# Two attention layers: all jobs in new orders, with row-major score jobs of different 32-row groups side by side

## The reference

```
# layer 0, per batch: channels on 128 rows, 256 positions, 16 heads of width 8
q = layer_norm(x + pos) @ Wq;  k, v = layer_norm(ctx + pos) @ Wk, Wv
probs = softmax(q k^T / sqrt(8));  x += (probs v) @ Wo;  then layer norm and a gelu feed-forward
# layer 1, per batch: 128 queries, 256 keys (context, then the tokens themselves), 16 heads of width 16
scores = q k^T * scale + mask;  x = rmsnorm(x + softmax(scores) v @ out_w);  then a gelu feed-forward
```

## Time and profile before

| what | value |
| --- | --- |
| median of 3 runs | 2342.38 us (2339.53 to 2348.45) |
| the profiled execution's own time | 2341.19 us |
| its span in the trace | 2339.3 us |
| PE busy | 2192.3 us, 94% of the span |
| DVE, ACT, POOL busy | 1476.0, 1316.3, 684.5 us |
| first layer's attention, PE at work | 13.3 to 335.4 us |
| second layer's attention, PE at work | 368.4 to about 645.2 us |

### The profile page before, as it was taken

One profiled execution on the slowest core, in us unless ns is written; L12 is line 12 of the kernel. 1 busy time (PEld: TensorE's weight loads), 2 busy tenths in 40 slices (PEclk: granted clock), 3 DMA queues, 4 the chain that ended last, 5 costly groups with the idle time before them and its releaser, 6 DMA issues. The chain is left out here.

```text
span 2339.3 us, 48273 instructions
## 1 busy us (share of the span) xinstructions
PE 2192.3 (94%) x18208; PEld 1805.4 (77%) x18208; DVE 1476.0 (63%) x2833; ACT 1316.3 (56%) x3812; POOL 684.5 (29%) x652
## 2 busy tenths in 40 slices
PE   6999978999888999999999999999999899999989
PEld 4666646777677888888888888888887786776778
DVE  5778743444463666566666766666666538999963
ACT  4777753454443544444445444444444549999953
POOL 4443312111170423030211503030101506677740
PEclk9999998999989999999999999999999899999999
DMA  4000002000011101010100001010000201000000
GB/s 131 16 15 11 2 1 55 2 2 2 2 37 46 39 25 37 1 46 1 30 17 10 30 17 37 1 37 1 1 1 1 109 21 37 2 2 2 2 10 28
DMA packets 33666, 50.62 MB, mean 22 GB/s; under 512 B 2592, under 2 KB 22048, under 8 KB 32416
## 3 DMA queue, kind: packets, MB, share of 16 engines
q1 hardware_dynamic: 33440, 47.53, 6.5%
HBM read 45.43 MB, written 2.10 MB: 20 GB/s over the span
## 5 line engine op out<-in xcount | busy, mean ns | idle before, releaser
L633 ACT ACTIVATE l_probs<-l_s_psum,l_neg_max 128x129 f32<-128x129 f32 x512 | 181.4, 367 | 266.3 <-DVE l_neg_max L696 266.3
L720 DVE TENSOR_TENSOR x<-x,l_o_psum 128x512 f32<-128x512 f32 x256 | 176.1, 688 | 189.1 <-PE l_o_psum L587 187.4
L2524 ACT ACTIVATE l_probs<-l_probs,l_neg_max 128x128 f32<-128x128 f32 x512 | 210.9, 534 | 0.0
L618 ACT ACTIVATE l_KT<-l_k_psum,cols 128x512 f32<-128x512 f32 x128 | 88.2, 689 | 196.9 <-PE l_k_psum L114 196.9
L465 POOL TENSOR_TENSOR l_head_w_high<-l_head_raw,one 128x768 fp32r<-128x768 f32 x30 | 44.5, 1482 | 516.2 <-PE l_o_psum L587 516.2
L1232 DVE TENSOR_REDUCE l_neg_max<-l_psum 128x2 f32<-128x512 f32 x256 | 164.5, 683 | 48.5 <-PE l_psum L1024 48.4
L2354 POOL TENSOR_TENSOR l_probs<-l_probs,l_mask_add 128x512 f32<-128x512 f32 x128 | 162.0, 1286 | 78.6 <-DVE l_probs L2582 78.6
L1163 ACT ACTIVATE l_PT<-l_psum 128x512 f32<-128x512 f32 x256 | 132.1, 603 | 56.5 <-PE l_psum L1052 53.8
L587 PE MATMUL l_o_psum<-l_head_w_high,l_context_low 128*128 128x256 f32 x512 | 155.8, 304 | 8.5 <-DVE l_context_low L701 8.5
L701 DVE SCALAR_TENSOR_TENSOR l_context_low<-l_c_psum,cols,l_context_high 128x512 fp32r<-128x512 f32 x128 | 95.8, 749 | 105.3 <-ACT l_context_high L625 104.5
L2524 ACT ACTIVATION_READ_ACCUMULATOR l_probs<-l_probs,l_neg_max 128x1 f32 x512 | 155.2, 334 | 0.0
(11 more groups left out here) (303 smaller groups left out, 6600.2 us busy)
## 6 DMA issues: line engine op xcount, KB each, us to landing
l_head_raw<-in_l_heads SPq DMA_DIRECT2D x32, 384.0 KB, 2.9
l_w<-in_l_w SPq DMA_DIRECT2D x4, 1024.0 KB, 9.8
l_ctx_in<-in_ctx_T SPq DMA_DIRECT2D x16, 256.0 KB, 5.5
l_value_raw<-in_l_values SPq DMA_DIRECT2D x8, 512.0 KB, 3.5
l_value_rows<-in_l_rows SPq DMA_DIRECT2D x8, 512.0 KB, 5.0
l_x_in<-in_x_T SPq DMA_DIRECT2D x16, 128.0 KB, 2.1
l_x_in<-in_ctx_T SPq DMA_DIRECT2D x16, 128.0 KB, 2.5
values<-in_l_w SPq DMA_DIRECT2D x2, 1024.0 KB, 5.9
```

The source lines that it names most:

```text
L633: last = act.activation(probs[:, i, :], scores[:, i // 2, i % 2, :], ACT.Exp, bias=neg_max[:, i:i + 1], scale=1.0, accum_out=den[:, i:i + 1])
L720: dve.tensor_tensor(out=x, in0=x, in1=o_bank[:, :], op=ALU.add).then_inc(o_free, 1)
L2524: last = act.activation(p, p, ACT.Exp, bias=neg_max[:, s % SCORES3, m:m + 1], scale=1.0, accum_out=den[:, u % 2, 4 * r + m:4 * r + m + 1])
```

## The change

Both tables get new numbers; no job is added, removed or altered. The core of the diff:

```diff
 AT0 = {
-    "rows": (0.62, 0.63, 0.68, 0.74, 0.77, 0.8, 0.84, 0.84,
-             0.86, 0.89, 1.02, 1.08, 1.17, 1.27, 1.3, 1.32),
+    "rows": (-0.69, -0.6899, -0.57, -0.5699, -0.48, -0.4799, -0.32, -0.3199,
+             -0.29, -0.2899, -0.27, -0.2699, -0.09, -0.0899, 0.09, 0.0901),
...
 AT1 = {
-    "rows": (-3.3, -2.91, -2.87, -2.6, -2.47, -2.4, -2.33, -2.33),
+    "rows": (-4.97, -4.95, -4.34, -4.25, -4, -4, -4, -4),
...
-    "neg_T_a": (-2.51,),
+    "neg_T_a": (-4.18,),
...
-    "exponents": (-2.48, -2.36, -2.35, -2.27, -2.03, -1.51, -1.51, -1.51),
+    "exponents": (-4.15, -4.11, -3.97, -3.97, -3.18, -3.18, -3.18, -3.18),
```

More of the change, by code:

```diff
@@ L762 @@
 AT0 = {
[L763 to L774, removed]
-    "rows": (0.62, 0.63, 0.68, 0.74, 0.77, 0.8, 0.84, 0.84,
-             0.86, 0.89, 1.02, 1.08, 1.17, 1.27, 1.3, 1.32),
[L777 to L799, removed]
+    "place": (-4.97,),
+    "stats": (-3.77,),
+    "root": (-3.79,),
+    "scaled": (-1.91,),
+    "normed": (-1.6,),
+    "normed_a": (-1.23,),
+    "project": (-0.98,),
+    "project_a": (-0.54,),
+    "round": (-1.43,),
+    "blocks": (-0.94,),
+    "value": (-0.72,),
+    "values": (-0.55,),
+    "rows": (-0.69, -0.6899, -0.57, -0.5699, -0.48, -0.4799, -0.32, -0.3199,
+             -0.29, -0.2899, -0.27, -0.2699, -0.09, -0.0899, 0.09, 0.0901),
+    "maximum": (-0.5, -0.46, -0.4, -0.39, -0.29, -0.21, -0.21, -0.15,
+             -0.1, -0.08, -0.07, -0.06, -0.03, 0.01, 0.03, 0.06),
+    "parts": (0.16,),
+    "neg_T": (0.23,),
+    "neg_T_a": (0.48,),
+    "score": (0.29, 0.46, 0.72, 0.88),
+    "exponents": (0.56, 0.57, 0.63, 0.68, 0.82, 0.92, 1.01, 1.01, 1.1, 1.12, 1.12, 1.18, 1.28, 1.28, 1.41, 1.42),
+    "context": (0.73, 1.16),
+    "slots": (1.22, 1.51),
+    "untangle": (1.35, 1.49),
+    "share": (1.58, 1.64),
+    "context_T": (1.57,),
+    "turned_T": (2.02,),
+    "out": (1.99,),
+    "added": (2.03,),
+    "back": (2.22,),
+    "back_a": (2.54,),
+    "stats_b": (2.84,),
+    "root_b": (2.32,),
+    "scaled_b": (3.29,),
+    "renormed": (3.43,),
+    "renormed_a": (3.73,),
 }
@@ L1297 @@
 AT1 = {
[L1298 to L1307, removed]
-    "rows": (-3.3, -2.91, -2.87, -2.6, -2.47, -2.4, -2.33, -2.33),
-    "maximum": (-3.85, -3.18, -3.05, -2.88, -2.88, -2.88, -2.88, -2.88),
-    "parts": (-2.87,),
-    "neg_T": (-2.02,),
-    "neg_T_a": (-2.51,),
-    "score": (-1.98, -1.37),
-    "exponents": (-2.48, -2.36, -2.35, -2.27, -2.03, -1.51, -1.51, -1.51),
[L1315 to L1327, removed]
+    "x_T": (-6.21,),
+    "x_T_a": (-6.67,),
+    "query": (-5.83,),
+    "query_a": (-6.17,),
+    "round_q": (-2.38,),
+    "key": (-5.53, -5.15),
+    "key_a": (-5.75, -5.49),
+    "round_k": (-1.83,),
+    "value": (-3.88,),
+    "values": (-6.46,),
+    "rows": (-4.97, -4.95, -4.34, -4.25, -4, -4, -4, -4),
+    "maximum": (-7.77, -7.66, -6.92, -6.86, -6.8, -6.8, -6.8, -6.8),
+    "parts": (-6.68,),
+    "neg_T": (-3.88,),
+    "neg_T_a": (-4.18,),
+    "score": (-3.64, -2.99),
+    "exponents": (-4.15, -4.11, -3.97, -3.97, -3.18, -3.18, -3.18, -3.18),
+    "context": (-2.79,),
+    "slots": (-3.17,),
+    "untangle": (-2.57,),
+    "share": (-5.18,),
+    "context_T": (-2.03,),
+    "turned_T": (-2.38,),
+    "out": (-1.12,),
+    "residual": (1.1,),
+    "added": (-3.85,),
+    "square": (-3.38,),
+    "root": (2.52,),
+    "scaled": (1.63,),
+    "normed": (2.28,),
     "normed_a": (1.84,),
```

## The result

The changed kernel takes 2357.91 us (median of 6 runs, 2353.13 to 2363.78) against 2344.78 us of the kernel before beside it. The ratio is 1.0059 with a 95% interval of 1.0044 to 1.0073: slower by 0.6%, where I had forecast 0.7% faster. The profiled executions differ by 16.8 us (spans 2356.1 and 2339.3).

A forecast was written before the change was run, and what follows sets the result against it. PE's jobs and waits were taken as the bound (PE busy 94% of the span). Terms 7 - 25 - 3 + 4 = -17 us, from 2341.19 us, gave a forecast of 2325 us, range 2304 to 2342 us.

The forecast's parts named there:

- First attention, +7 us for 14 items: First attention: an item lengthens from 18.05 to 18.6 us, taken as +0.5 us an item, +7 us for 14 items.
- the walk: First attention: one item's new order stepped through with durations from the old profile's rows, ending at 18.6 us.
- The rival of the other side: First attention: items wait for the chain maxima, share, `context_T`, maxima; 21.2 us an item, +44 us, 2362 us; chance 0.07.
- 16.9 us: First attention: lower end for an item, eight pairs in 8 slots with nothing waiting, -16 us in all.
- Second attention, -25 us: Second attention, item 2's first score half to item 14's: new order with paired rows jobs takes 171.3 us against 196.4.
- the tie: Second attention: exponents precede copy `neg_T_a` up to item 8, copy first from item 9; then waits of 2.6 and 0.7 us.
- the two waits: Second attention, items 13 and 14: two PE waits of 2.6 us, included in their 26.8 us.
- Three pairs of 27.6 less 0.6: Second attention, items 3 to 8: three pairs of 27.6 us, less 0.6 for one `normed` not yet there; 82.1 us.
- Filling and draining, -3 us: Second attention: filling and draining the pipeline saves a few slots each, -3 us.
- The clock, +4 us: Second attention and tail: about six PE waits of 2.5 us; one or two lower-clock stretches beyond the tail's own, +4 us.

The follow-up runs named there:

- experiment 11: The changed kernel with GpSimd's rounding, position addition and `blocks` in the first attention each issued as four quarter-size instructions; 2324.89 us, ratio 0.9921.
- experiment 9: experiment 1 plus the copy move of experiment 6, and VectorE's `scaled_b` moved ahead of the parts (3.155 for 3.29); 2304.88 us, ratio 0.9834.
- experiment 1: The changed kernel with one added wait: GpSimd's rounding of item u starts only after VectorE made the parts of item u-1; 2330.88 us, ratio 0.9956.
- experiment 10: experiment 9 with the first attention's sixteen row-major score jobs renumbered so four in a row use the same 32 TensorE rows; 2312.69 us, ratio 0.9860.
- experiment 6: experiment 2 with the copy `neg_T_a` moved behind the exponents in every item (-4.175 for -4.18); 2304.07 us, ratio 0.9835.
- experiment 2: The kernel before with only the second attention's new order; 2327.32 us, ratio 0.9930.
- experiment 3: The kernel before with only the first attention's new order; 2380.19 us, ratio 1.0153.
- experiment 4: The kernel before with VectorE's parts placed behind the statistics of item u+4 in the first attention, so they fall into GpSimd's rounding; 2357.01 us, ratio 1.0058.

## Why the prediction was wrong, point by point

- **First attention, +7 us for 14 items: measured +35.7** (+37.3 with the first). The step that failed is the walk: it gave each instruction its duration from a row of the kernel before and moved it along its own engine, with `parts` among the things that needed no word. I never laid POOL's row beside DVE's at the new place. The two items of 19.04 us in the kernel before, with 1.78 us for an instruction of 0.19, showed the price, and I passed over them. In its place the runs show that the two instructions of 0.18 and 0.19 us last 1.25 and 1.19 to 1.83 us beside GpSimd, PE waits 1.77 to 2.41 us for them in every item, and part of the waits bring the lower clock. With little or nothing of this the walk was near: 18.6 us forecast, 18.43 in experiment 11 and 18.07 in experiment 9.
- **The rival of the other side** named nearly the right item (21.2 us) and time (2362), and got 0.07. Its mechanism is refuted: experiments 1, 9 and 11 leave all maxima and shares in their order.
- **The Trainium skill, TensorEngine Tiling (Array Packing), section PSUM Bottleneck**, for which I didn't take 16.9 us. By that page I expected no gain. The traces bear that out for the new order as a whole (18.07 us in experiment 9, 18.05 before), but not for the pairs by themselves: in the first attention they are worth 0.5 us an item (experiment 10).
- **Second attention, -25 us: measured -21.7** for the same stretch (174.7 us against 171.3 forecast). Pairs of 27.2 us (forecast 27.6) up to item 8 and 31.8 (31.2) from there to item 12, with waits of 2.4 us (2.6) at L1595 in six items. The mechanism was right in each part, also that of the tie (experiment 6). The size was off where `query` and `key` are gone: items 13 and 14 take 29.9 us, where I had 26.8. Without waits, in experiment 6, they take 25.0 us, so the two waits were right and the work under them was too small by 3 us. (Three pairs of 27.6 less 0.6 are 82.2 and not 82.1 us, a slip that changes nothing; measured 81.2.)
- **Filling and draining, -3 us: measured about +3,** of which +3.4 us is the stretch ahead of the second attention, by its lower clock (see experiments 2 and 3). A gain of 3 us shows nowhere.
- **The clock, +4 us.** I had looked for it in the second attention alone, where four stretches of 3.4 us came up to its end. The first had eleven, by my estimate 13 us.
- The range ended at 2342 because the other side was held for a matter of DVE's chain. No case in it had POOL in it.

## What to carry to other kernels

When an order moves a short VectorE instruction that reads SBUF twice, or casts from SBUF to SBUF, lay GpSimd's timeline beside it at the new place: it costs what is left of the GpSimd instruction that runs then. Rare long instances of a short instruction in a trace (here 1.78 us beside 0.19) show this price before the change is made. Where the collision can't be ordered away, one wait on GpSimd or GpSimd instructions of a quarter of the size take most of it back (27 and 33 us here). And where two executions differ by a few us in a stretch that no edit touches, compare the granted clock of that stretch first.

## What was not expected of the hardware

- The block is strict and repeats: the second short instruction, ready some 0.1 us after GpSimd's next one has started, waits for all of that too (137.99 to 139.18), so 0.37 us of work became 2.44 us.
- A cast of 32 elements a partition is blocked like an instruction with two inputs (experiment 4: 1.27 us); the statistics (0.86 us for four at 139.11) and a copy from PSUM (0.41 us at 131.07 in experiment 1) are not slowed.
- The wait alone doesn't tell whether the clock falls. It fell for 3.4 us after a wait of 1.77 us amid full work (0.50 from 140.10 to 143.30) and stayed up after three of 2.41 us in the same kernel; with waits of up to 1.1 us it stayed at 1.00 from 54 to 325 us (experiment 4), and in experiments 9 and 10 it fell twice and three times between 54 and 300 us without a wait above 0.36 us.
